# Two attentions on one core: context loads and key stores move ahead of other stores on SyncE's queue

## The chip, the cores and the metric

The kernel runs on one core of a Trainium2 chip, as one launch. The metric is the device time of that launch in microseconds. The kernel before takes 874.25 us, the median of three runs (872.12 to 876.36).

Engine names are those of the profile: PE multiplies matrices (PEld is its weight load), DVE is VectorE, ACT is ScalarE, POOL is GpSimd, SP is SyncE. SP issues most DMAs here. It works through one list of instructions in order: where it meets a semaphore wait, everything behind the wait stands.

## What is computed

Two layers work on `x` [16, 100, 256], with a context `ctx_1024` [16, 361, 256]:

```python
x = x + tanh(g_xattn[0]) * L0_xattn(layernorm(x), ctx, mask)   # 16 heads of 16, bias on q, k, v, o
x = x + tanh(g_ffn[0])   * L0_ffn(layernorm(x))                # 8 experts, top 2, and a shared one
x = x + tanh(g_xattn[1]) * L1_xattn(layernorm(x), ctx)         # no mask, no bias but b_o
x = x + tanh(g_ffn[1])   * L1_ffn(layernorm(x))                # 8 LoRA experts, top 1

# both cross-attentions, for each batch b:
q = ln(x) @ Wq;  k = ctx @ Wk;  v = ctx @ Wv
out = softmax(q k^T / sqrt(16)) v @ Wo
```

Everything is float32 to the caller.

## The kernel before

The kernel is written by hand engine by engine: each engine has its own instruction stream and all order between engines is by semaphores. The two attentions share their code; `l` is 0 or 1. Batches are numbered 0 to 15, and buffers that hold one batch's data exist twice (`cT[n % 2]`, `KS[n % 2]`, `QS[n % 2]`, `V1[n % 2]`).

**What a batch needs.** `ctx_load(l, n, p)` (L384) brings the transposed context of batch n, 361 KB, into `cT[p]`. PE projects it to keys (`project_k`, L2067, two halves m) and to values (`project_v`, L2085, three tiles of rows). Keys are kept as three bfloat16 parts for accuracy: ACT writes the first (`k_first`, L973), DVE the remainder `kr` (`k_rest`, L1555), ACT the second (`k_second`), POOL the third (`k3`, L724). They lie in one buffer `kp`, so ACT's `k_first` of batch n waits until the store of the keys of n-1 has landed. `k_store(l, n)` (L400) stores `kp` to the scratch tensor `scr_k` in three DMAs of 180.5 KB, each behind the wait for its part. `k_load` (L415) brings them back in the layout that the scores want, as two halves of three DMAs each into `KS`, behind a wait for the store (half 0). Queries go the same way: `q_store(l, g)` (L472) stores one group in six DMAs, `q_load` (L463) brings the queries of one batch into `QS` behind a wait for that store. A group is four batches in the first attention and two in the second. `max_load` (L519) brings the negated row maxima into `QS`, behind ACT's copy `mp`.

`ctx_load` waits for `v_ready` >= START + 2(n-1): the values of batch n-2, which used the same buffer, are projected.

**The steady state.** Step b (PE: L2166) holds the transposed scores and the weighted sum of batch b, the scores and maxima of batch b+1, the values of batch b+2 (tiles 0 and 1 at the end of step b, tile 2 near the start of step b+1) and the keys of batch b+3 (in the second half). Steps have u = b % 2: "odd steps" are those with u = 1. SP's step (L544) is: context b+3; in even steps 2 to 12 of the second attention the store of query group b/2 + 1; k_load and q_load of b+2, half 0; max_load of b+1 and a wait for its landing; k_load and q_load of b+2, half 1; the masks (first attention); the key store of b+3.

**The prologues.** SP's `attn` (L577) writes out the order of the first batches. First attention: ... context 2, Wo, q_store(0), q_store(1), k_store(1), loads of keys and queries 1, small vectors, max_load(0), k_store(2), masks 2, q_store(2), step 0. Second: ... context 2, k_store(1), q_store(0), loads of keys and queries 1, max_load(0), k_store(2), q_store(1), step 0. In both, DVE computes `kr` of keys 2 and then `cTl`, the low part of context 1 (`ctx_low`, L1548), which PE's values 1 wait for; DVE then takes the last maxima of batch 0 and splits them, and PE transposes them (`turn_max`, L2109) between tiles 1 and 2 of values 1.

The profile gives matrix multiplications issued through `split_mm` the line L1962.

Of the kernel before, what the change touches and what calls it, by code (L numbers as in the profile page):

```python
# [15 lines left out]
B, S, S2, D, H = 16, 100, 361, 256, 16  # L16
# [54 lines left out]
def build(nc, io, out):  # L71
    ctx = ExitStack()
    with ctx:
# [309 lines left out]
        def _(sp):  # L383
# [135 lines left out]
            def max_load(l, n, p):  # L519

                sp.wait_ge(sa[l]["mp"], START + n + 1)
                sp.sem_inc(s_held, 1)
                sp.dma_start(QS[p][SROWS:KSROWS, :, :], mp[:, :]).then_inc(sd["mload"][p], 16)
# [18 lines left out]
                sp.dma_start(woT[:, t:t + 2, :], io["woT"].rearrange("(t p) n -> p t n", p=P)[:, t:t + 2, :]).then_inc(s_wf[1], 16)  # L542

            def step(l, b, u, i, has_ctx, has_k, weights=None):  # L544
                if has_ctx:
                    ctx_load(l, b + 3, 1 - u, False)
                if l == 1 and u == 0 and 2 <= b <= 12:
                    q_store(l, b // 2 + 1)
                if has_k:
                    k_load(l, b + 2, 0)  # L550
                    q_load(l, b + 2, 0)
                    if l == 0 and b == 0:
                        q_store(l, 3)
                    if l == 0 and weights is not None:
                        expert_up(weights, u)
                        expert_down(weights, u)
                    if l == 1 and 8 <= b < 12:
                        inner_weights(b - 8)
                    if l == 1 and b == 12:
                        outer_weights(0)  # L560
                        outer_weights(1)
                    max_load(l, b + 1, 1 - u)
                    sp.wait_ge(sd["mload"][1 - u], 16 * (i + u + 1))
                    sp.sem_inc(s_held, 1)
                    k_load(l, b + 2, 1)
                    q_load(l, b + 2, 1)
                    if l == 1 and b == 13:
                        outer_weights(2)
                        outer_weights(3)
                        for r in range(LPROD):  # L570
                            sp.dma_start(BT[r * LR:(r + 1) * LR, :], io["loraBT"]).then_inc(s_wf[1], 16)
                if l == 0 and has_ctx:
                    mask_load(b + 3, 1 - u, False)
                if has_ctx:
                    k_store(l, b + 3)

            def attn(l):  # L577
# [14 lines left out]
                if l == 0:  # L592
                    for part in range(NPIECE):
                        first_keys(part, (0, 1))
                    first_queries(l, 0)
                    first_queries(l, 1)
                    ctx_load(l, 2, 0, False)
                    sp.dma_start(w_attn[0]["o"][:, :, :], io["L0_xattn_Wo"].rearrange("(k p) n -> p k n", p=P)).then_inc(s_wa[0]["o"], 16)
                    restore_rows(l)
                    q_store(l, 0)  # L600
                    q_store(l, 1)
                    k_store(l, 1)
                else:
                    k_store(l, 0)
                    for half in range(2):
                        k_load(l, 0, half)
                    first_queries(l, 0)
                    ctx_load(l, 2, 0, False)
                    first_queries(l, 1, (1, 2))
                    k_store(l, 1)  # L610
                    q_store(l, 0)
# [3 lines left out]
                if l == 0:  # L615
                    small_vectors()
                max_load(l, 0, 0)
                k_store(l, 2)
                if l == 0:
                    mask_load(2, 0, False)  # L620
# [1973 lines left out]
```

## Time and profile before

| | |
|---|---|
| median of three runs | 874.25 us (872.12 to 876.36) |
| the profiled execution | 885.38 us, its span 883.2 us |
| mean granted TensorE clock in it | 0.953 |
| PE busy | 790.0 us, 89% of the span |
| DVE, ACT, POOL busy | 577.6, 472.0, 213.8 us |
| DMA | 117.85 MB, mean 133 GB/s |
| idle PE before `project_k`, released by a context's landing | 9.9 us, 10 times |
| idle ACT before `kp`, released by the landing of `scr_k` | 5.7 us, once |

The first attention runs from the start to about 320 us, its feed-forward layer to 466, the second attention to about 765, the last feed-forward layer to the end. Stretches of time in the rows are in us from the start of the span. "Released by" is what ended an idle time. In a row in order of time the figures are start, duration, engine, line, operation, output and input; a bracket at the end is the idle time before it. Rows of matrix multiplications that overlap are merged, and ends are modelled.

### The profile page before, as it was taken

To read this page: it belongs to the slowest core of one execution; us is meant where nothing else is said; L and a number is where in the kernel's file an instruction comes from. 1 tells how busy PE (TensorE), PEld (TensorE's weight loads), DVE (VectorE), ACT (ScalarE), POOL (GpSimd) and SP (SyncE) were. 2 spreads that over 40 slices of the span, in tenths; PEclk is the share of its full clock that TensorE was granted. 3 is DMA by queue.
4 is the path that set the end of the run, shared out by engine and by line. 5 is a ranking of instruction groups with operands and counts; after the bars stand their busy time and mean duration, and the time that the engine had idled before them with its cause. 6 is when DMAs were issued, how large, how long until landed. Compare 5 with 4: busy or idle time off the path is not lost.

```text
span 883.2 us, 22331 instructions
## 1 busy us (share of the span) xinstructions
PE 790.0 (89%) x7992; PEld 608.7 (69%) x7992; DVE 577.6 (65%) x1773; ACT 472.0 (53%) x1012; POOL 213.8 (24%) x212
## 2 busy tenths in 40 slices
PE   5869999999999887799997788999999889898996
PEld 2546777777767664489974566776776667576996
DVE  3757777777777766465546767778788657564332
ACT  2436566556556566246652455666566555654553
POOL 2535132133223306400026522332221111000000
PEclk9889999999999999799997889999999999799998
DMA  7698878878886906523326958699789877000001
GB/s 195 159 192 189 171 150 169 160 152 179 160 175 131 221 2 174 147 75 120 121 75 161 175 126 171 139 184 176 149 176 187 159 172 165 2 1 1 19 19 37
DMA packets 153754, 117.85 MB, mean 133 GB/s; under 512 B 81564, under 2 KB 145160, under 8 KB 153640
## 3 DMA queue, kind: packets, MB, share of 16 engines
q1 hardware_dynamic: 146400, 107.93, 57.1%
q0 software_dynamic: 4096, 6.57, 3.0%
q10 hardware_dynamic: 3152, 1.96, 0.9%
q8 instruction: 64, 1.05, 0.6%
q14 instruction: 42, 0.34, 0.2%
HBM read 76.17 MB, written 38.30 MB: 130 GB/s over the span
## 4 chain that ended last, share of the span: by engine, by line
PE 57%; DMA 15%; SPq 9%; DVE 7%; issue 4%; ACT 4%; ACTq 1%; another core or an unknown queue 1%; POOL 0%; DVEq 0%
PE ps L1962 18%; PE ps L2080 7%; DMA cT<-in_ctxT 7%; PE ps L2106 5%; PE ps L2139 4%; PE ps L2129 4%; DMA scr_q<-qp 3%; SPq L477 3%; DMA QS<-mp 3%; PE ps L2400 3%; PE ps L2125 3%; SPq L426 2%; PE ps L2163 2%; SPq L413 2%; PE ps L2033 2%
## 5 line engine op out<-in xcount | busy, mean ns | idle before, releaser
L1017 ACT ACTIVATE prob<-ps 128x400 f32<-128x400 f32 (+1 forms) x384 | 182.5, 500 | 96.3 <-PE ps L2129 83.0
L2106 PE MATMUL ps<-KS,QS 96*100 96x361 bf16 x512 | 166.3, 341 | 17.0 <-DMA QS<-scr_q 5.8
L1575 DVE CUSTOM_DVE_ANT_0 ps<-ps,biasq 100x361 f32<-100x361 f32 x256 | 135.4, 543 | 52.1 <-PE ps L2106 48.4
L1579 DVE TENSOR_REDUCE mx<-ps 100x1 f32<-100x361 f32 x256 | 127.4, 528 | 59.4 <-PE ps L2106 56.6
L2129 PEld LDWEIGHTS ps<-QS,KS 98*128 98x128 bf16 x1536 | 109.3, 100 | 50.1 <-issue 10.8
L2129 PE MATMUL ps<-QS,KS 98*128 98x100 bf16 x1536 | 134.0, 211 | 6.0 <-ACT prob L1017 3.8
L2080 PE MATMUL ps<-cT,wk 128*128 128x361 f32 x256 | 102.5, 512 | 17.6 <-DMA cT<-in_ctxT 9.9
L2106 PEld LDWEIGHTS ps<-KS,QS 96*100 96x100 bf16 x512 | 64.1, 127 | 54.7 <-DVE mx L1579 13.4
L727 POOL TENSOR_TENSOR kp<-kr,kp 128x722 bf16<-128x722 f32 x32 | 48.7, 1523 | 195.9 <-ACT kp L988 195.6
L2139 PE MATMUL ps<-prob,V 128*17 128x100 f32 (+1 forms) x3072 | 80.4, 253 | 1.4 <-ACT xT L908 1.4
L2139 PEld LDWEIGHTS ps<-prob,V 128*17 128x17 f32 (+1 forms) x3072 | 65.1, 98 | 12.9 <-issue 8.0
L2080 PEld LDWEIGHTS ps<-cT,wk 128*128 128x128 f32 x256 | 48.8, 207 | 36.4 <-issue 14.9
L1962 PE MATMUL ps<-wvh,cTh 128*128 128x256 f32 x192 | 61.5, 320 | 5.9 <-DVE cTl L1552 5.4
L2125 PE MATMUL ps<-biasT,ident_bf 128*128 128x400 bf16 (+1 forms) x192 | 64.2, 334 | 2.0 <-ACT prob L1017 1.8
L983 ACT ACTIVATE kp<-ps,bk 128x361 bf16<-128x361 f32 x64 | 35.3, 554 | 55.3 <-PE ps L2080 46.9
L848 POOL DMA_INDIRECT scr_x<-xn,posi x32 | 33.3, 1041 | 93.8 <-PE ps L2139 87.0
L1962 PE MATMUL ps<-wvl,cTh 128*128 128x256 f32 x192 | 55.1, 287 | 0.0
L1962 PE MATMUL ps<-wvh,cTl 128*128 128x256 f32 x192 | 55.0, 287 | 0.0
L1560 DVE SCALAR_TENSOR_TENSOR kr<-ps,bk,kp 128x361 f32<-128x361 f32 x64 | 37.7, 592 | 22.6 <-ACT kp L983 21.9
L1824 DVE TENSOR_TENSOR hlo<-hh,hhi 128x400 fp32r<-128x400 f32 x32 | 18.4, 575 | 49.2 <-ACT hhi L1262 49.1
L1962 PEld LDWEIGHTS ps<-wvh,cTh 128*128 128x128 f32 x192 | 37.6, 196 | 12.1 <-DVE kr L1560 6.1
L1834 DVE TENSOR_TENSOR hx<-ps,sg 128x192 f32<-128x192 f32 (+1 forms) x48 | 17.1, 357 | 42.9 <-ACT sg L1183 36.3
(225 smaller groups left out, 1612.9 us busy)
## 6 DMA issues: line engine op xcount, KB each, us to landing
scr_k<-kp SPq DMA_DIRECT2D x93, 180.5 KB
KS<-scr_k SPq DMA_DIRECT2D x62, 270.8 KB
cT<-in_ctxT SPq DMA_DIRECT2D x32, 361.0 KB
KS<-scr_k SPq DMA_DIRECT2D x62, 180.5 KB
QS<-scr_q SPq DMA_DIRECT2D x60, 150.0 KB
KS<-scr_k SPq DMA_DIRECT2D x62, 90.2 KB
scr_q<-qp SPq DMA_DIRECT2D x42, 100.0 KB, 6.6
xg<-scr_x SPq DMA_DIRECT2D x32, 128.0 KB
```

What stands on the lines that cost most here:

```text
L727: nc.gpsimd.tensor_tensor(kp[:, 2, :, :], kr[:, :, :], kp[:, 1, :, :], ALU.subtract).then_inc(a["k3"], 1)
L983: nc.scalar.activation(kp[:, 0, m, :], ps[:, key_bank(l, n, m), 0:S2], ACT.Identity, bias=bk[l][:, m:m + 1]).then_inc(a["k1"], 1)
L1017: nc.scalar.activation(prob[0:KROWS[t], t, hg, :], ps[0:KROWS[t], c % 2, 0:HQ * S], ACT.Exp).then_inc(a["exp"], 1)
L1560: nc.vector.scalar_tensor_tensor(kr[:, m, :], ps[:, key_bank(l, n, m), 0:S2], bk[l][:, m:m + 1], kp[:, 0, m, :], ALU.add, ALU.subtract).th ...
L1575: nc.vector.tensor_tensor_reduce(ps[0:S, banks[h % len(banks)], 0:S2], ps[0:S, banks[h % len(banks)], 0:S2], biasq[p][:, :], 1.0, -3.0e38, ...
L1579: nc.vector.reduce_max(mx[:, h:h + 1], ps[0:S, banks[h % len(banks)], 0:S2], axis=AX.X).then_inc(a["max"], 1)
L1962: x = mm(dst, w_parts[wp], x_parts[xp], start=first and j == 0, stop=last and j == 2)
L2080: x = mm(ps[:, key_bank(l, n, m), 0:S2], w_attn[l]["k"][:, k, m * P:(m + 1) * P], cT[p][:, k, 0:S2], start=k == 0, stop=k == KT - 1)
L2106: mm(ps[0:S, banks[h % len(banks)], 0:S2], QS[p][0:SROWS, h, :], KS[p][0:SROWS, h * S2:(h + 1) * S2], start=True, stop=True).then_inc(a["s ...
L2125: mm(dst, ident_bf[0:rows, :], bc(biasT[p][0:rows, t, :].unsqueeze(1), [rows, HQ, S]), start=True, stop=False)
L2129: x = mm(ps[:, c % 2, j * S:(j + 1) * S], KS[p][:, h * S2 + t * P:h * S2 + (t + 1) * P], QS[p][:, h, :], start=l == 1, stop=l == 1 or j == ...
L2139: x = mm(ps[32 * j:32 * j + HD + 1, 6, hg * S:(hg + 1) * S], V1[p][0:KROWS[t], t, HQ * hg + j, :], prob[0:KROWS[t], t, hg, j * S:(j + 1) * ...
```

## The change

Three things change on SP's list, and nothing on any other engine. The same DMAs are issued, with the same waits and sizes.

In the prologue of the first attention k_store(1) stands ahead of q_store(1). In both prologues context 3 is loaded behind max_load(0), ahead of k_store(2), and no longer at the start of step 0. In the second attention an odd-numbered context b+4 is loaded at the end of the odd step b, ahead of its key store, and no longer at the start of the even step b+1. Even-numbered contexts there, and all contexts after number 3 in the first attention, stay where they were.

```diff
             def step(l, b, u, i, has_ctx, has_k, weights=None):
-                if has_ctx:
+                if has_ctx and b > 0 and (l == 0 or u == 1):
                     ctx_load(l, b + 3, 1 - u, False)
...
                 if l == 0 and has_ctx:
                     mask_load(b + 3, 1 - u, False)
+                if l == 1 and u == 1 and b + 4 < B:
+                    ctx_load(l, b + 4, u, False)
                 if has_ctx:
                     k_store(l, b + 3)
...
                     q_store(l, 0)
+                    k_store(l, 1)
                     q_store(l, 1)
-                    k_store(l, 1)
                 else:
...
                 max_load(l, 0, 0)
+                ctx_load(l, 3, 1, False)
                 k_store(l, 2)
```

## Rows read from the trace of the kernel before

**Rows 1.** The chain of waits, 30 to 62 us: start, duration, what.
```profile
43.94 4.68 DMA scr_k<-kp
...
51.42 2.90 PE ps L1962 x12
...
54.49 1.33 PE ps L1962 x6
```

**Rows 2.** SP's instructions in order of time, 39.5 to 44.6 us.
```profile
39.03 3.70 SPq L477 DMA_DIRECT2D scr_q<-qp  x7
42.84 1.55 SPq L413 DMA_DIRECT2D scr_k<-kp  x3
```

**Rows 3.** POOL, ACT, DVE and PE in order of time, 38 to 54 us.
```profile
38.56 1.46 POOL L727 TENSOR_TENSOR kp<-kr,kp 128x722 bf16<-128x722 f32 x1 [1.88 <-ACT kp L988]
...
42.11 0.84 ACT L891 ACTIVATE xT<-ps 128x800 f32<-128x800 f32 x1 [1.97 <-PE ps L1974]
...
45.91 0.14 DVE L1575 DVE_READ_ACCUMULATOR2_ANT mx<- 100x1 f32 x1
49.32 1.09 DVE L1560 SCALAR_TENSOR_TENSOR kr<-ps,bk,kp 128x361 f32<-128x361 f32 x2 [3.27 <-ACT kp L983]
...
53.59 0.17 DVE L1589 SCALAR_TENSOR_TENSOR mxs<-mx,mxb 100x16 f32<-100x16 f32 x1
...
51.42 0.55 PE L1962 MATMUL ps<-wvh,cTh 128*128 128x256 f32 x1 [4.53 <-DVE cTl L1552]
```

**Rows 4.** Busy time by stretch; after the engines: granted clock, DMA share, GB/s.
```profile
38.00:40.00 2.00, 2.00 (x9) 1.18 (x8) 2.00 (x9) 2.00 (x4) 1.44 (x2) 1.00 0.37 99
44.00:46.00 2.00, 2.00 (x8) 1.10 (x7) 1.64 (x8) 0.00 (x0) 0.00 (x0) 1.00 1.08 307
52.00:54.00 2.00, 2.00 (x11) 2.00 (x11) 1.93 (x10) 0.31 (x2) 0.80 (x1) 0.50 1.21 178
```

**Rows 5.** PE's first key projection of steps 0, 2, 6 and 12, second attention.
```profile
510.50 1.57 PE L2080 MATMUL ps<-cT,wk 128*128 128x361 f32 x2 [1.85 <-DMA cT<-in_ctxT]
...
547.47 0.88 PE L2080 MATMUL ps<-cT,wk 128*128 128x361 f32 x2 [2.60 <-DMA cT<-in_ctxT]
...
616.12 0.87 PE L2080 MATMUL ps<-cT,wk 128*128 128x361 f32 x2 [0.45 <-DMA cT<-in_ctxT]
...
719.22 1.57 PE L2080 MATMUL ps<-cT,wk 128*128 128x361 f32 x2 [1.45 <-DMA cT<-in_ctxT]
```

**Rows 6.** SP in order of time around context 3 and in step 2; PE's values 3.
```profile
501.78 0.61 SPq L390 DMA_DIRECT2D cT<-in_ctxT  x1
...
537.17 1.58 SPq L413 DMA_DIRECT2D scr_k<-kp  x3
539.04 0.58 SPq L390 DMA_DIRECT2D cT<-in_ctxT  x1
539.67 3.59 SPq L477 DMA_DIRECT2D scr_q<-qp  x6
...
550.09 0.57 SPq L469 DMA_DIRECT2D QS<-scr_q  x1
...
538.67 0.28 PE L1962 MATMUL ps<-wvh,cTl 128*128 128x256 f32 x1
```

**Rows 7.** The chain of waits, 514 to 522 us: values at the full clock.
```profile
517.82 1.62 PE ps L1962 x12
```

**Rows 8.** Busy time by stretch, 608 to 620 us; columns as in rows 4.
```profile
608.00:620.00 12.00, 11.29 (x115) 7.84 (x119) 9.96 (x25) 7.07 (x17) 3.15 (x5) 1.00 1.13 220
```

**Rows 9.** The chain of waits in step 6 of the second attention.
```profile
613.52 6.75 DMA scr_q<-qp
...
620.36 3.10 DMA QS<-scr_q
```

**Rows 10.** SP and ACT in order of time in step 6, 612 to 624 us.
```profile
615.58 1.25 SPq L426 DMA_DIRECT2D KS<-scr_k  x3
...
617.86 0.57 ACT L983 ACTIVATE kp<-ps,bk 128x361 bf16<-128x361 f32 x1 [1.87 <-PE ps L2080]
```

## The prediction

> **What bounds the kernel now.** I read the page first: PE is busy for 89% of the span, so only a stretch in which PE stands still or runs at the lower clock can give time back. The list of busy times does not say where those are. The chain of work that ended last does. In the first 60 us it does not stay on PE: it goes from SP's query stores to the store of the second batch's keys, the landing of that store, one ScalarE copy, two VectorE steps, and only then to PE's value projection [rows 1]. Then I read the lists in order of time around the three places that the diff touches: the prologue of the first attention, that of the second, and the steps of the second.
>
> The prologue of the first attention. The store of keys 1 begins at 42.84, behind seven query stores that hold SP from 39.03 to 42.73, the last of q_store(0) and all six of q_store(1) [rows 2]. Its last part, issued at 43.94, lands 4.68 us later [rows 1]. ScalarE has been free since 42.95; VectorE stands 3.27 us for ScalarE's copy, and PE 4.53 us for VectorE [rows 3]. PE then works at half of the full clock (0.50 granted, the 1.2 GHz level) [rows 4].
>
> The second attention. PE waits for a context at 510.50 (1.85 us, step 0), 547.47 (2.60, step 2), 616.12 (0.45, step 6) and 719.22 (1.45, step 12) [rows 5]. All four are odd-numbered contexts, those that even steps load. Their issue lies right behind a key store: in step 2 keys from 537.17, the context at 539.04, six query stores from 539.67 [rows 6].
>
> **The change part by part. (a) Keys 1 ahead of queries 1, first attention.** Nothing is added; three DMA issues move ahead of six. The six take 42.73 less 39.03, times six sevenths, 3.2 us, so k_store(1) begins at about 39.6. Its third part needs POOL's subtraction, done at 38.56+1.46 = 40.02 [rows 3], and its issue would come at 40.7, so SP does not stand. When does it land? The DMA engines were at share 0.37 in 38 to 40 and at 1.08 and 307 GB/s in 44 to 46 [rows 4]: at 39.6 the queue is nearly empty. 541 KB at 307 GB/s are 1.8 us, and the last part is issued at 40.7, so its bytes are through at about 41.6. Before, bytes still ran at full rate up to 46, and the landing was at 48.62, at most 2.6 us later. So the landing comes at 44.2 or sooner. ScalarE is free at 42.95 and copies at about 44. Now VectorE is late instead: its maxima run until 45.91+0.14 = 46.05, and its kr step started at 49.32. **It starts 3.27 us earlier, bound by VectorE and no longer by the store**; the landing has 1.3 us of room before it would matter again. PE's wait of 4.53 becomes 1.26.
>
> The clock is the second term. With a stand of 1.26 instead of 4.53 I expect the full clock. 12 value matmuls take 2.90 us here [rows 1] and 1.62 at the full clock [rows 7]. The transposition of the maxima then has to wait for VectorE, 53.59+0.17-3.27 = 50.49 [rows 3], and PE goes on at 50.6 with the last 6 matmuls (1.33 here, 0.8 at the full clock), ending at 51.4 where they ended at 55.82 [rows 1]. **Sum of (a): 4.4 us**, or 3.3 if the clock falls anyway. What the query matmuls behind them save is some tenths and left out.
>
> On this the Trainium skill ("TensorE: Matmul & The Clock Gate", What's actually happening) says that the array is throttled by default and released by activity, and that the point of a change of level varies from run to run. By its rule PE keeps 2.4 GHz here or pays a low stretch elsewhere; the second gives 3.3. The row agrees with the first half: 0.50 after the long stand.
>
> What is queued behind: q_store(1) now ends at about 44.4, where k_store(1) ended. Its landing is wanted by q_first(3), after 55 in this trace; no cost. k_load(1), which waited for the landing, goes out at 44.5 instead of 48.7, and the small vectors, max_load(0) and keys 2 come four us earlier with it. That is needed, since PE is there over four us earlier.
>
> **(b) First context 3 ahead of k_store(2).** In the first attention the list shows no idle stretch of PE before keys 3; k_store(2) leaves 0.6 us later (a context takes 0.58 to issue [rows 6]), hidden by the wait of the k_load behind it for PE. Zero. In the second, the load leaves before three key stores (1.58) and six query stores (3.59) [rows 6], so at about 496.5 instead of 501.78. Its own wait, for values 1, is met within 1 us of max_load(0) ahead of it, which needs a transposition that PE does in the middle of them. It lands well before 510.50-1.85 = 508.65, where PE wants it. **Gain 1.85 us** [rows 5].
>
> **(c) Odd contexts ahead of the odd steps' key stores, second attention.** Here a wait moves with the issue. The load waits for the end of a value projection, which PE reaches inside its next step: 538.67+0.28 = 538.95 for the load of 539.04 [rows 6]. It cannot go out earlier than now. The key store, ready at 537.17, is held back by that wait and one issue, 2.5 us, and the query stores behind it by its three issues, 1.6. What is won is the place in the DMA queue: 541 KB of keys no longer precede 361 KB of context. In 608 to 620 the engines are saturated, at share 1.13 [rows 8]. At 220 GB/s the context lands 541/220 = 2.5 us earlier and the keys 361/220 = 1.6 us later.
>
> Step 2: the wait of 2.60 goes. But then another chain is late next: query stores, their landing, q_load, its landing, the next step's scores. In step 6 that is 613.52 plus 6.75, 620.36 plus 3.10 [rows 9], and PE starts its next step at 616.12+7.4 = 623.5, just as it lands. In step 2 q_load goes at 550.09 [rows 6], landing at 553.2; PE, coming 7.4 us and 1.3 of low clock after 547.47, was at 556.2. Now PE could be there at 552.3 and the load at 553.2 to 553.8. **Gain 2.5 us.** In step 12, by the same chain, I take **0.5** of 1.45. Steps 4, 6, 8, 10: waits of 0 to 0.45 go, but they are at the chain already, and each loses 0.5 us net: the query stores leave 1.6 later into a full queue, which absorbs most of it, and ScalarE's copy of the next keys, which waits for the key store's landing, wants it at 617.86 and would have it at 615.58+1.6 = 617.2 or later [rows 10]. **Loss 2.0**; the bounds of one such step are 0 (all absorbed) and 1.6 (none).
>
> **Sum**: 4.4 + 1.85 + 2.5 + 0.5 - 2.0 = 7.3 us. The profiled execution took 885.38 us (span 883.2, 2.2 around it), so it would take 878.1. It lies 11 us over the median 874.25, but the terms that are plain waits (3.27, 1.85, 2.60) do not hang on that. Against the median: 874.25 - 7.3 = **866.9**.
>
> **The rivals.** *Give-back*: (a) and (b) hold, but steps 2 to 12 lose the whole 1.6 us of the query stores' delay: 6 x 1.6 = 9.6 against 4.4 + 1.85 + 2.5. Time about 875, no change. For it: the chain of step 6 has no slack. Against: the engines there are saturated, so bytes and not issues set the landing. *Slower*: the held key store stalls ScalarE, and the exponentials queued behind its copy stop, and PE with them. In step 6 keys 8 had landed by 615.58, 2.3 us before the copy [rows 10]. If the delays add up (2.5 of issue and 1.6 of bytes) instead of overlapping, each of six steps stalls about 2 us, and such stands cost some 1.3 us of clock each, as 12 matmuls lose 2.90-1.62: 20 us, less 3.3 and 1.85: 889. It decides once the keys land over 2.3 us later than now. *The order of issue does not set the landing*: contexts land when they did, and (c) is only the loss of 2.0. 4.4 + 1.85 - 2.0 = 4.2, time 870. The Trainium skill ("DMA: Bandwidth & Descriptors", Queues, rings and completion order) says that descriptors of a ring are consumed in order while completion is not first in, first out. The landings of step 6 speak against the rival: keys by 615.58, context 616.12, queries 620.27, in the order of issue [rows 5, 9, 10]. *More*: nothing is given back and the clock holds too, with 1.3 us in each of steps 0 and 2: 4.4 + 3.15 + 3.9 + 1.45 = 12.9, time 861.4.
>
> **How the numbers follow.** Forecast 0.57, give-back 0.17, order without effect 0.07, more 0.13, slower 0.06. Range: 859 (more, with the 2 us by which the runs of before spread) to 874 (forecast and the lower half of give-back). A measurement of this kernel tells about 0.5%, 4.4 us, from no change: the line is at 869.9. Faster: the forecast, more and a little of the order case, 0.73. Within: 0.20. Slower: 0.07.
>
> **What would show it.** (a) VectorE's wait for ScalarE's copy gone, kr at about 46, PE's wait about 1.3, granted clock 1 behind it, values 1 done near 51.4. (b) No wait for a context at keys 3 of the second attention. (c) Waits for odd contexts under 0.3 us, the key store right behind the load, its landing some 2 us later, perhaps short ScalarE waits for it, more waits for queries at the start of odd steps. The prediction is wrong if step 0 of the first attention then waits for max_load or keys 1 as long as PE did before, or if the even steps of the second lose over 1.5 us each.

## The result, and the profile after

| | before | after |
|---|---|---|
| median, 20 runs each | 877.68 us (872.12 to 883.82) | 882.89 us (875.98 to 893.67) |
| ratio, 95% interval | | 1.0049 [1.0028, 1.0071] |
| profiled execution, its span | 885.38, 883.2 us | 893.67, 891.5 us |
| mean granted clock in it | 0.953 | 0.951 |

The change makes the kernel half a per cent slower, 4 to 5 us. The prediction said 7 us faster, and its range (859 to 874) does not hold the time. Of the 16.0 us between its 866.9 and 882.89, 3.4 are its starting point: the median of before was 874.25 over three runs and is 877.68 over twenty. The two profiled executions lie 7.7 and 10.8 us above the medians of their kernels, so they are read here for what happens in a step, and the sizes come from the ratios.

The table of idle times before PE's work moved from one line to the other. Before, PE lost 9.9 us in 10 waits for contexts. After, 2.0 us in 2 waits are left, both in the first attention, and these have grown:

```profile
PE ps L2109 <- DMA QS<-scr_q: 15.7, 10, 2.4
...
PE ps L1989 <- DVE xn L1334: 6.2, 8, 2.7
```

(Waits of PE after: line, what was waited for, us in total, times, longest. L2109 is the score, which was L2106 and had 5.8 us in 10 waits.) In the second attention PE no longer waits for contexts, it waits for queries. On SP the wait for the projected values, L389, grew to four times its length. First before, then after:

```profile
SPq L389 <- PE ps L1962: 5.0, 8, 1.5
```
```profile
SPq L389 <- PE ps L1965: 21.3, 13, 2.5
```

**The first prologue after.** ACT, DVE and PE in order of time, in answer to [rows 3], and SP to [rows 2]:

```profile
38.96 1.51 SPq L413 DMA_DIRECT2D scr_k<-kp  x3
40.52 3.20 SPq L477 DMA_DIRECT2D scr_q<-qp  x6
...
44.82 1.02 ACT L986 ACTIVATE kp<-ps,bk 128x361 bf16<-128x361 f32 x2 [2.20 <-DMA scr_k<-kp]
...
45.58 1.09 DVE L1563 SCALAR_TENSOR_TENSOR kr<-ps,bk,kp 128x361 f32<-128x361 f32 x2
...
47.68 0.36 PE L1965 MATMUL ps<-wvh,cTh 128*128 128x256 f32 x1 [1.11 <-DVE cTl L1555]
...
55.57 1.08 PE L2334 MATMUL ps<-wo,onT 128*100 128x256 f32 x4 [1.40 <-issue]
```

The keys go out first, ACT copies at 44.82, VectorE's `kr` follows its maxima with no wait, and PE stands 1.11 us instead of 4.53. The product with Wo starts at 55.57; before it was at 60.52, in the row of the same form

```profile
60.52 1.08 PE L2331 MATMUL ps<-wo,onT 128*100 128x256 f32 x4 [1.40 <-issue]
```

so 4.95 us are won up to there. Of that 4.0 us are still there at keys 3, 1.3 at keys 5 and 1.2 at keys 15 of the first attention. The clock did hold in 48 to 50 (1.00), but fell behind, as the second and third line of the busy times by stretch show (after the engines: granted clock, DMA share, GB/s):

```profile
48.00:50.00 2.00, 1.35 (x12) 1.15 (x10) 1.93 (x11) 0.57 (x2) 1.05 (x1) 1.00 0.98 182
...
60.00:62.00 2.00, 2.00 (x15) 1.30 (x14) 1.44 (x7) 1.61 (x4) 2.00 (x2) 0.61 1.13 260
62.00:64.00 2.00, 2.00 (x13) 1.14 (x11) 1.26 (x5) 1.13 (x4) 2.00 (x2) 0.53 1.12 320
```

**Step 6 of the second attention after.** SP in order of time, in answer to [rows 9, 10], from the second half of the loads of queries 7 to the load of queries 8:

```profile
609.80 0.57 SPq L469 DMA_DIRECT2D QS<-scr_q  x1
612.17 0.57 SPq L390 DMA_DIRECT2D cT<-in_ctxT  x1
612.94 1.55 SPq L413 DMA_DIRECT2D scr_k<-kp  x3
614.54 3.96 SPq L477 DMA_DIRECT2D scr_q<-qp  x6
620.13 2.21 SPq L426 DMA_DIRECT2D KS<-scr_k  x3
624.06 0.58 SPq L469 DMA_DIRECT2D QS<-scr_q  x1
```

The same piece of SP's list before:

```profile
607.39 0.58 SPq L469 DMA_DIRECT2D QS<-scr_q  x1
608.16 1.56 SPq L413 DMA_DIRECT2D scr_k<-kp  x3
609.84 0.58 SPq L390 DMA_DIRECT2D cT<-in_ctxT  x1
610.47 3.61 SPq L477 DMA_DIRECT2D scr_q<-qp  x6
615.58 1.25 SPq L426 DMA_DIRECT2D KS<-scr_k  x3
620.36 0.57 SPq L469 DMA_DIRECT2D QS<-scr_q  x1
```

From the first line to the last are 12.97 us before and 14.26 after. After, SP stands with nothing issued from 610.4 to 612.17, since the context's wait is now ahead of everything else. PE pays for it at the start of the next step, and its clock falls (PE in order of time, and busy time by stretch):

```profile
627.05 0.84 PE L2109 MATMUL ps<-KS,QS 96*100 96x361 bf16 x2 [2.21 <-DMA QS<-scr_q]
```
```profile
624.00:626.00 2.00, 0.84 (x8) 0.63 (x6) 1.10 (x3) 1.30 (x3) 1.60 (x1) 1.00 0.28 56
626.00:628.00 2.00, 0.95 (x4) 0.76 (x5) 0.37 (x1) 0.00 (x0) 1.51 (x3) 0.77 0.39 58
628.00:630.00 2.00, 2.00 (x9) 1.99 (x8) 0.60 (x2) 0.00 (x0) 1.82 (x2) 0.50 1.01 209
```

The odd steps 3 to 13 after begin with six such waits: 2.28, 2.37, 2.21, 2.20, 1.87 and 2.02 us. A seventh, of 0.95 us, lies within step 12.

### The profile page after: what moved, and what is told of

Same layout as the page of the kernel before. It is cut to its first block, busy times and chain, and to the rows that moved or that the text cites. A ratio compares the mean times of both kernels' runs of the same rounds, so it can differ in the third digit from the quotient of the medians.

```text
span 891.5 us, 22331 instructions
## 1 busy us (share of the span) xinstructions
PE 790.3 (89%) x7992; PEld 615.2 (69%) x7992; DVE 581.8 (65%) x1773; ACT 472.6 (53%) x1012; POOL 215.9 (24%) x212
## 3 DMA queue, kind: packets, MB, share of 16 engines
q8 instruction: 64, 1.05, 0.5%
## 4 chain that ended last, share of the span: by engine, by line
PE 56%; DMA 13%; DVE 10%; SPq 10%; issue 5%; ACT 4%; POOL 1%; DVEq 0%; ACTq 0%; POOLq 0%
PE ps L1965 18%; PE ps L2109 6%; PE ps L2083 6%; DMA scr_q<-qp 5%; PE ps L2132 5%; PE ps L2142 4%; SPq L477 3%; DMA QS<-scr_q 3%; PE ps L2166 2%; PE ps L2128 2%; DMA cT<-in_ctxT 2%; SPq L413 2%; PE ps L2024 2%; DMA QS<-mp 2%; DVE mx L1582 1%
## 5 line engine op out<-in xcount | busy, mean ns | idle before, releaser
L2109 PE MATMUL ps<-KS,QS 96*100 96x361 bf16 x512 | 169.1, 346 | 28.4 <-DMA QS<-scr_q 15.7
L2132 PEld LDWEIGHTS ps<-QS,KS 98*128 98x128 bf16 x1536 | 111.3, 102 | 54.0 <-issue 10.1
L2132 PE MATMUL ps<-QS,KS 98*128 98x100 bf16 x1536 | 136.4, 213 | 9.2 <-ACT prob L1020 4.9
L2109 PEld LDWEIGHTS ps<-KS,QS 96*100 96x100 bf16 x512 | 65.1, 129 | 65.0 <-DMA QS<-scr_q 17.2
L2083 PE MATMUL ps<-cT,wk 128*128 128x361 f32 x256 | 98.9, 497 | 9.5 <-PEq L2374 6.8
L851 POOL DMA_INDIRECT scr_x<-xn,posi x32 | 36.0, 1125 | 94.0 <-PE ps L2142 87.2
## 6 DMA issues: line engine op xcount, KB each, us to landing
scr_k<-kp SPq DMA_DIRECT2D x93, 180.5 KB, 5.2
KS<-scr_k SPq DMA_DIRECT2D x62, 180.5 KB, 4.2
```

The costliest lines, as they stand in the source:

```text
L851: nc.gpsimd.indirect_dma_start(scr_x, bass.IndirectOffsetOnAxis(posi[:, c, b:b + 1], 0), normalized(b), None).then_inc(s_scat, 16)
L2083: x = mm(ps[:, key_bank(l, n, m), 0:S2], w_attn[l]["k"][:, k, m * P:(m + 1) * P], cT[p][:, k, 0:S2], start=k == 0, stop=k == KT - 1)
L2109: mm(ps[0:S, banks[h % len(banks)], 0:S2], QS[p][0:SROWS, h, :], KS[p][0:SROWS, h * S2:(h + 1) * S2], start=True, stop=True).then_inc(a["s ...
L2132: x = mm(ps[:, c % 2, j * S:(j + 1) * S], KS[p][:, h * S2 + t * P:h * S2 + (t + 1) * P], QS[p][:, h, :], start=l == 1, stop=l == 1 or j == ...
```

## The experiments

**The parts one by one.** Four kernels each hold one part of the change, or two.

e1_a, part (a) alone:

```diff
                     q_store(l, 0)
+                    k_store(l, 1)
                     q_store(l, 1)
-                    k_store(l, 1)
```

> The kernel before with one edit: k_store(1) ahead of q_store(1) in the prologue of the first attention. Theory 'the prologue gain holds': PE reaches the Wo product of the prologue 4.9 us earlier, as in the trace of the changed kernel (55.57 against 60.52), and the whole kernel is 4 to 5 us faster, ratio 0.995. Theory 'eaten inside the first attention': the first scores are as early, but the keys of steps 1 to 3 give it back (in the changed kernel 4.0 us at keys 3, 3.2 at keys 4, 1.3 at keys 5, 0.7 to 1.2 at keys 14 and 15), and the kernel is 0.5 to 1.5 us faster, ratio 0.998 to 1.

Measured: 0.9988 [0.9950, 1.0027], medians 874.48 and 877.45. The mechanism is there as in the change, PE's wait is 2.20 us (46.11, for `cTl`) instead of 4.53, but the time is not to be told from no change.

e2_ab, parts (a) and (b), the steps of the second attention as before:

```diff
             def step(l, b, u, i, has_ctx, has_k, weights=None):
-                if has_ctx:
+                if has_ctx and b > 0:
                     ctx_load(l, b + 3, 1 - u, False)
...
                 max_load(l, 0, 0)
+                ctx_load(l, 3, 1, False)
                 k_store(l, 2)
```

> Keys 1 ahead of queries 1, and context 3 ahead of k_store(2) in both prologues; the odd contexts of the second attention stay at the start of even steps. Theory 'the queries' chain is the cost': without the held key stores the loss is gone, no wait for QS over 1 us at the start of an odd step, and the kernel is 1 to 4 us faster than before. Theory 'the early context is part of the cost' (it delays the landing of max_load(0), or a DVE step collides): slower than the kernel with keys 1 alone by 1 us or more, with PE waiting over 2 us between 495 and 510 again, as in the changed kernel (3.33 and 2.67).

Measured: 0.9981 [0.9939, 1.0022]. The point is a gain of 1.7 us; the 6.25 us that the prediction gave to both parts would be 0.9929, just outside.

e3_c, part (c) alone: the two lines of the diff for the odd contexts of the second attention, nothing in the prologues.

```diff
+                if l == 1 and u == 1 and b + 4 < B:
+                    ctx_load(l, b + 4, u, False)
                 if has_ctx:
                     k_store(l, b + 3)
```

> Only the odd contexts of the second attention move, ahead of the odd steps' key stores. Theory 'the queries' chain is the cost': PE gains 2.6 us at keys 5 and loses about 2.2 us at the start of each of the steps 3, 5, 7, 9, 11, with a low stretch of the clock behind each, 9 us from keys 5 to keys 15 as in the changed kernel; the kernel is 6 to 8 us slower than before, ratio 1.007 to 1.009. Rival 'the loss comes from the other edits or from the clock alone': within 2 us of before.

Measured: 1.0119 [1.0066, 1.0172]. This part alone loses 10 us, more than the whole change does, where the prediction had a gain of 1.0.

e4_b1, part (b) in the second attention alone.

```diff
                 max_load(l, 0, 0)
+                if l == 1:
+                    ctx_load(l, 3, 1, False)
                 k_store(l, 2)
```

> Only context 3 of the second attention moves ahead of k_store(2). Theory 'a wait saved': the 1.85 us wait at keys 3 goes and keys 3 start 1 to 2 us earlier against the start of the second attention, kernel 1 to 3 us faster. Rival 'another wait takes its place': as in the changed kernel PE waits over 2 us for xn or for the maxima's load and keys 3 start no earlier; kernel the same within 1 us.

Measured: 1.0006 [0.9963, 1.0049]: nothing, though the wait of 1.85 us is gone.

**What in part (c) costs: the held store or the order of the bytes?** e5_hold leaves the loads where they were and only makes SP wait, ahead of the odd steps' key store, for the event for which the moved context load waits. (The `sem_inc` is a free counter that nobody reads.)

```diff
+                if l == 1 and u == 1 and b + 4 < B:
+                    sp.wait_ge(sa[l]["v_ready"], START + 2 * (b + 3))
+                    sp.sem_inc(s_held, 1)
                 if has_ctx:
                     k_store(l, b + 3)
```

> The kernel before, all loads where they were; in the odd steps 1 to 11 of the second attention SP waits ahead of the key store for the value projection that the following context load waits for anyway. So the key store, and all behind it, leave as late as with the moved contexts, but nothing stands in front of the keys in the DMA queue. Theory 'the hold is the cost': the query stores leave 1.8 to 2.2 us later, the stands at the start of odd steps are as long as with the moved contexts or longer (2 us and more), the contexts land later as well, and the kernel is 8 to 14 us slower, ratio 1.01 or more. Rival 'the bytes of the context ahead of the keys are the cost': 0 to 3 us slower.

Measured: 1.0079 [1.0044, 1.0115]. The hold by itself, with the order of all transfers unchanged, costs time. But half of what was expected did not come: the stands of 2 us for queries at the start of odd steps are missing. PE's waits for queries are 1.11 us at most from step 2 on, and it stands for the odd contexts instead, which the hold delays here too, for 1.99, 1.73, 1.85, 0.69, 0.38 and 1.28 us:

```profile
PE ps L2083 <- DMA cT<-in_ctxT: 9.8, 11, 2.0
```

So this loss reaches PE another way than that of part (c), and the run does not say which share of part (c)'s loss is the hold.

Then the queries, whose lateness is what PE feels in the change, were moved forward. e6_c_q_before_k is part (c) with the order context, queries, keys:

```diff
-                if l == 1 and u == 0 and 2 <= b <= 12:
-                    q_store(l, b // 2 + 1)
...
+                if l == 1 and u == 1 and 1 <= b <= 11:
+                    q_store(l, (b + 1) // 2 + 1)
                 if has_ctx:
                     k_store(l, b + 3)
```

> Odd contexts moved as in the change, and the six query stores of an even step moved with them, to between the context load and the key store. The queries then leave as early after the context as before the change, the key store 3.6 us later still. Theory 'the queries' chain is the cost': the stands for QS at the start of odd steps fall under 1 us, unless the keys' store takes their place: ScalarE's copy of the next keys waits for its landing (here 3 to 4 us longer) and k_load too; I expect ratio 1.00 to 1.01. Theory 'the key store's landing is the cost': ScalarE waits 3 us and more per even step, PE stands behind it, ratio over 1.012.

Measured: 1.0190 [1.0138, 1.0241]. PE's waits for queries fall to 8.0 us in all, but now the keys are late and ScalarE stands, six times for 3.8 to 4.8 us in the second attention:

```profile
619.08 0.57 ACT L985 ACTIVATE kp<-ps,bk 128x361 bf16<-128x361 f32 x1 [4.81 <-DMA scr_k<-kp]
```

In the change itself the waits of this kind are 1.4 to 2.7 us in the second attention. Before, ScalarE stood for PE at the same places: 1.3 to 1.9 us in steps 4 to 10, over 4 us in steps 2 and 12.

e7_c_q_early has the order queries, context, keys, all in the odd step (the stores of the even step are taken out as in e6):

```diff
+                if l == 1 and u == 1 and 1 <= b <= 11:
+                    q_store(l, (b + 1) // 2 + 1)
                 if l == 1 and u == 1 and b + 4 < B:
                     ctx_load(l, b + 4, u, False)
```

> Odd contexts moved as in the change, and the query stores moved ahead of them, into the stretch in which SP would stand for the value projection (the queries' third part is ready 6 us before). Order in an odd step: query stores, context, key store. Theory 'the queries' chain is the cost': the stands for QS are gone, keys 5 start 2 us and more earlier, the contexts may wait for 600 KB of queries (up to 2.7 us); ratio 0.992 to 1.000. Rival 'the held key store is the cost': still slower than before by 5 us or more.

Measured: 1.0158 [1.0118, 1.0198]. The six query stores are in the queue during the hold, so a queue with work in it is not enough: contexts are as late as before (11.4 us of PE's waits) and ScalarE waits 23.8 us for keys.

e8_q_early is the kernel before with only the query stores moved to the odd step, ahead of the key store; nothing is held.

```diff
-                if l == 1 and u == 0 and 2 <= b <= 12:
-                    q_store(l, b // 2 + 1)
...
+                if l == 1 and u == 1 and 1 <= b <= 11:
+                    q_store(l, (b + 1) // 2 + 1)
                 if has_ctx:
                     k_store(l, b + 3)
```

> The kernel before, with the query stores of the even steps moved to the odd step before, ahead of its key store; contexts stay. Theory 'the queries' chain is what is late in the even steps': the small stands for QS of the kernel before (0.27, 0.34, 0.88 us) go, but key store and context leave 3.6 us later behind the query stores, and PE stands for the context in even steps by 1 to 3 us: ratio 0.998 to 1.006. If the chain had slack and only the hold made it late, this kernel shows no gain at all.

Measured: 1.0251 [1.0205, 1.0297], the slowest of all, and far outside what was expected. No wait for queries is left in the steps, and PE waits for contexts instead:

```profile
PE ps L2080 <- DMA cT<-in_ctxT: 21.7, 8, 3.9
```

In these three kernels each transfer that was put ahead took its time from another one that PE or ScalarE then stood for.

**Taking away the hole.** If SP's stand is what costs, keys that are issued ahead of it must save the loss. e10_two_parts_first is part (c), but two of the three parts of the keys go ahead of the context and the third behind it. PE gets its odd contexts early all the same. (The lines stand against e3_c, and `k_store` now takes the parts that it stores.)

```diff
                 if l == 1 and u == 1 and b + 4 < B:
+                    k_store(l, b + 3, range(2))
                     ctx_load(l, b + 4, u, False)
-                if has_ctx:
+                    k_store(l, b + 3, range(2, 3))
+                elif has_ctx:
                     k_store(l, b + 3)
```

> The moved contexts of the change (second attention only), but two of the three parts of the keys go ahead of the context; only the third part and what follows it are held. The prologues are as before. Theory 'the DMA engines run dry during the hold': with two parts of 181 KB in the queue they do not, so the bytes are through earlier; the stands for QS at the start of odd steps fall from 2.2 to about 1.2 us and the loss from 1.2% to about 0.5%. Rival 'the six query stores are issued later, and that is all': they leave only 1 us earlier than with the whole store held, loss 0.8 to 1.2%.

Measured: 0.9990 [0.9958, 1.0022]. The whole loss of part (c) is gone. What differs between the two kernels is when two DMAs of 180.5 KB are issued.

The rival of the expectation, the issue time on SP alone, is part of it: the two issues take 1.01 us in which SP would have stood, and the queries are stored 4.02 us after the last query load (mean of the even steps 2 to 12), against 4.99 in e3_c. It is not all of it: the next query load leaves 1.7 us earlier than in e3_c, and even 0.4 us earlier than in e1, e2 and e4, where these steps are untouched and the queries are stored at 3.55. A third thing goes as well: in e3_c ScalarE waits six times, 10.0 us in all, for the landing of keys in the steps of the second attention, and here never. The runs do not tell what each of the three is worth.

e15_one_part_first sends one part ahead (`range(1)` and `range(1, 3)` in the same diff):

> Part (c) alone, with one of the three parts of the keys issued ahead of the context and two behind it: a dose between the two kernels run so far (no part ahead: 1.0119; two parts ahead: 0.999). Theory of the hole: one part is 180 KB, at 220 to 300 GB/s 0.6 to 0.8 us of transfer, against a hole of some 2 us, so about a third to a half of the loss goes: 1.004 to 1.009, and the load of queries of the next step leaves at about 13.0 us behind the half-1 load in step 6 (no part ahead 13.59, two ahead 12.26). Rival (it is the late landing of the last part that counts, whatever the queue holds): as with two parts ahead, 0.996 to 1.002, or as with none, 1.010 to 1.014.

Measured: 1.0023 [0.9985, 1.0060], against 1.0119 and 0.9990. It lies between, nearer to two parts than I expected: by the middle values one part of keys saves 0.96 of 1.19%, not a third to a half, but the intervals are wide enough for a half. From the half-1 load to the next query load at step 6 are 13.23 us, where 13.0 was expected.

The DMA engines show what happens to the queue. Busy time by stretch (last two numbers: DMA share, GB/s) of the change, with the hold from 610.4 to 612.17:

```profile
609.00:611.00 2.00, 1.84 (x20) 1.47 (x19) 1.92 (x7) 1.30 (x4) 1.92 (x3) 1.00 0.96 214
611.00:613.00 2.00, 1.99 (x23) 1.67 (x21) 1.76 (x6) 1.70 (x5) 1.53 (x2) 1.00 0.99 144
613.00:615.00 2.00, 1.85 (x13) 1.32 (x14) 2.00 (x6) 1.50 (x4) 1.03 (x1) 1.00 0.63 128
615.00:617.00 2.00, 2.00 (x38) 1.27 (x36) 1.37 (x4) 1.01 (x3) 0.00 (x0) 1.00 1.07 340
```

The same place in the kernel before:

```profile
609.00:611.00 2.00, 1.90 (x20) 1.48 (x19) 1.77 (x5) 1.70 (x6) 1.48 (x3) 1.00 1.11 191
611.00:613.00 2.00, 1.94 (x14) 1.37 (x14) 1.81 (x5) 1.08 (x3) 0.76 (x1) 1.00 1.20 177
613.00:615.00 2.00, 1.90 (x37) 1.21 (x35) 1.64 (x4) 1.31 (x4) 0.00 (x0) 1.00 1.11 229
```

and in e10_two_parts_first, SP's list and the stretches:

```profile
599.13 0.58 SPq L469 DMA_DIRECT2D QS<-scr_q  x1
599.89 1.01 SPq L413 DMA_DIRECT2D scr_k<-kp  x2
601.70 0.84 SPq L390 DMA_DIRECT2D cT<-in_ctxT  x1
602.64 0.54 SPq L413 DMA_DIRECT2D scr_k<-kp  x1
```
```profile
601.00:603.00 2.00, 1.90 (x23) 1.49 (x21) 1.80 (x5) 1.70 (x5) 1.53 (x2) 1.00 1.09 197
603.00:605.00 2.00, 1.94 (x14) 1.21 (x11) 1.57 (x5) 1.26 (x4) 0.60 (x1) 1.00 1.06 230
```

About 3 us after SP stops issuing, the change's DMA share falls to 0.63, and in e3_c to 0.70 (612 to 614). Where two parts of keys are in the queue, and SP stands for 0.8 us instead of 1.8, it stays at 1.06 or more. That is the hole.

e14_change_two_parts_first is the whole change with this one difference:

> The whole change, but in the odd steps of the second attention two of the three parts of the keys are issued ahead of the odd context and only the third behind it. Theory (the loss is the hole in the DMA queue while SP stands for the end of the value projection with nothing issued): the loss of the change goes, as it went with part (c) alone, and what is left is the small gain of (a) and (b): ratio 0.995 to 1.000. From one half-1 load of queries to the next load of queries at step 6 about 12.3 us, where the change has 14.26. Rival (the changed order of bytes or the collisions in the second prologue make the loss, not the hold): 1.004 or more, as the change itself.

Measured: 0.9957 [0.9916, 0.9998], 869.0 against 872.89. The change as it stands is at 1.0049 [1.0028, 1.0071]; moving two DMA issues in front of a wait, in each of six odd steps, is worth 0.9%. This is also the fastest version tried. Its interval leaves 1 out by very little, so that it beats the kernel before is likely and not more; that it beats the change is clear.

**Are early contexts worth anything?** e11_c5_only moves the context of step 2 alone, the one where PE had waited longest:

```diff
+                if l == 1 and u == 1 and b == 1:
+                    ctx_load(l, b + 4, u, False)
                 if has_ctx:
                     k_store(l, b + 3)
```

> Only context 5 moves, the one for which PE waited longest (2.60 us in the trace of before; 1.7 to 2.2 in the traces of two other kernels with this stretch unchanged). Theory 'the query chain takes the wait over at once': keys 5 start 1.5 to 2.5 us earlier, step 3 begins no earlier or later by up to 2 us behind a stand of 2 us for QS; kernel 0 to 2 us slower. The prediction's theory: 2.5 us faster.

Measured: 1.0016 [0.9971, 1.0062]. The place where the prediction saw 2.5 us gives none that can be measured, though the interval just reaches that gain. In the trace PE does not wait for context 5, and step 3 begins with a stand of 1.66 us for queries. From keys 4 to keys 6 are 34.34 us, and 34.02 to 36.07 in e1, e2 and e4.

e12_odd_ctx_on_act and e13_a_all_ctx_on_act take the loads off SP, so that no wait for values holds anything on SP's list. ScalarE issues them behind its copy of the values: the odd contexts 5 to 15 in the first, contexts 4 to 15 and part (a) in the second.

```diff
-                if has_ctx:
+                if has_ctx and not (l == 1 and b > 0 and u == 0):
                     ctx_load(l, b + 3, 1 - u, False)
...
                 if has_b:
                     v_copy(l, b + 1, 1 - u, 1)
+                if (l == 1 and b > 0 and u == 0) and b + 3 < B:
+                    act.wait_ge(sa[l]["v_ready"], START + 2 * (b + 2))
+                    act.dma_start(cT[1 - u][:, :, 0:S2], io["ctxT"][b + 3]).then_inc(sd["ctx"][1 - u], 16)
```

> The kernel before, but the odd contexts 5 to 15 of the second attention are issued by ScalarE on its own DMA queue, right behind its copy of the last value tile, which waits for the same event as the load. SP is held by nothing and issues one DMA less. Theory 'holding SP was the cost of an early context, its place ahead of the keys was not': no wait of PE for an odd context, stands for QS as small as before, 3 to 7 us faster, ratio 0.992 to 0.997. Rival 'the engines have no bytes to spare: a context that comes earlier makes keys and queries land later by as much': waits for contexts go, stands for QS of 1 us and more appear, ratio 0.998 to 1.005. ScalarE gives up some 0.6 us per even step for the issue; if that shows, PE waits for prob.

Measured: 1.0028 [0.9994, 1.0063].

> Keys 1 ahead of queries 1 in the first prologue, and all contexts 4 to 15 of the second attention issued by ScalarE. Theory as in the run with the odd ones: the prologue's 1 to 3 us and 4 to 8 us in the second attention, since the even contexts (waits of 0.3 to 1 us per step) come earlier too: ratio 0.988 to 0.995. Rival: within 0.4% of before.

Measured: 0.9990 [0.9954, 1.0025]. In e12 PE's waits for contexts fell to 4.5 us in 5 places and those for queries to 3.9 us in 6, and the time did not. Part of the waits stayed: for context 5 alone PE waited 2.48 us in e12 and 3.21 us in e13. No kernel here shows that a wait for a context, once taken away, gives its length back.

**All of them by two numbers of the trace.** The first is the time from the last load of queries of one step to the first of the next, on SP, mean of the even steps 2 to 12. The second is PE's time from the start of keys 6 to that of keys 15, nine steps of the second attention.

| kernel | ratio | query load to query load | keys 6 to 15 |
|---|---|---|---|
| before | 1 | 12.77 | 153.5 |
| e1_a | 0.9988 | 12.54 | 150.9 |
| e2_ab | 0.9981 | 12.49 | 149.7 |
| e4_b1 | 1.0006 | 12.59 | 151.3 |
| e10, two parts ahead | 0.9990 | 12.15 | 147.5 |
| e14, change with two parts ahead | 0.9957 | 12.53 | 149.3 |
| e15, one part ahead | 1.0023 | 12.96 | 150.8 |
| e5_hold | 1.0079 | 13.25 | 155.1 |
| e3_c | 1.0119 | 13.86 | 157.3 |
| after | 1.0049 | 14.19 | 159.5 |
| e11_c5_only | 1.0016 | 12.46 | 148.6 |
| e12_odd_ctx_on_act | 1.0028 | 12.16 | 148.3 |
| e13_a_all_ctx_on_act | 0.9990 | 12.27 | 149.4 |
| e6, queries before keys | 1.0190 | 14.21 | 161.6 |
| e7, queries, context, keys | 1.0158 | 13.37 | 159.7 |
| e8_q_early | 1.0251 | 12.44 | 169.1 |

The last column for after is 725.77 less 566.25, in the rows of PE's first key projection

```profile
566.25 0.77 PE L2083 MATMUL ps<-cT,wk 128*128 128x361 f32 x2
...
725.77 0.77 PE L2083 MATMUL ps<-cT,wk 128*128 128x361 f32 x2
```

and for before 719.22 [rows 5] less the start of

```profile
565.74 0.88 PE L2080 MATMUL ps<-cT,wk 128*128 128x361 f32 x2
```

Each is one execution, and that of before took 7.7 us more than its median: e1, e2 and e4, which leave these steps alone, take 150.6 on average. Apart from the last three rows a later query load goes with longer steps, in rough order. The last three break it: there PE or ScalarE stands for contexts or keys. In e8 the query load is early and the steps are the longest of all.

## Why the prediction was wrong

**The bound.** That the first prologue hangs on the store of keys 1 was right: with the store early, PE's product comes 4.95 us sooner. That PE's waits for contexts in the second attention set its time was not. They were visible idle time, but the query chain stood right behind them, and the prediction charged it 0.5 us a step, in steps 4 to 10 alone. The trace also had four waits for even contexts, 0.42 to 0.95 us, which no part of the change touches.

**(a), 4.4 us: right in mechanism, too large as a term.** The store began at 38.96 (39.6 said), `kr` at 45.58 (46.05), PE's wait was 1.11 (1.26), the clock held behind it, and 4.95 us were won at the Wo product. Only the landing, at 44.8, came later than the 44.2 named as its latest: the last part was issued at 40.04, so it took 4.8 us, as long as before (4.68). The queue was not as empty as the prediction took it to be: the DMA share was 0.64 in 38 to 40 and 1.08 in 40 to 42. The run of this part alone measured 1.05 us of gain, [-2.4, 4.4]. Two things shrink the term. First, the trace of before was an uncommonly bad one at this place: from the second half of keys 2 to the Wo product it takes 21.6 us, the ten other kernels with the old order here take 19.2 to 21.0, the five with the new one 17.0 to 18.1, so the saving at that point is about 2.8 on average. Second, it shrinks on the way: over the same traces 2.4 are left at keys 3, 1.8 at keys 5 and 1.45 at keys 15. In the trace of after PE waits 1.53 us for context 4 at 84.38, and the granted clock is 0.61 and 0.53 in 60 to 64, where it was 1.00 before; its low stretch was in 50 to 58 then. The Trainium skill ("TensorE: Matmul & The Clock Gate", What's actually happening) says that the point of a change of level varies from run to run. The rows fit that in part: e1, e2 and e14, with the early store too, have their low stretch in 58 to 64 as well, and e13 has none there. With the fallen clock the prediction had 3.3, still above what was measured.

**(b), 1.85 us: the wait went, the time did not.** The context was issued at 496.09 (about 496.5 said) and PE no longer waits for it. But in the trace of after two other waits of PE in this prologue are longer (POOL, DVE and PE in order of time):

```profile
499.74 0.51 PE L2132 MATMUL ps<-QS,KS 98*128 98x100 bf16 x4 [3.33 <-DMA QS<-mp]
...
503.61 2.48 POOL L742 TENSOR_TENSOR x_sb<-x_sb,gbo 100x512 f32<-100x512 f32 x2
...
502.95 3.65 DVE L1334 TENSOR_SCALAR xn<-x_sb,mean_var,rstd 100x256 f32<-100x256 f32 x2
...
506.40 0.90 PE L1989 MATMUL ps<-ident,xn 100*128 100x100 f32 x4 [2.67 <-DVE xn L1334]
```

The first was 1.50 in the trace of before, but it is 2.0 to 3.3 in eleven of the fourteen other kernels, also in those with an untouched prologue (3.06 in e3_c); here the one trace of before was a good one. It averages 3.0 in the four kernels that hold part (b) and 2.2 in the twelve that do not, so the early context may be behind some of it; no run shows that by itself. The second is a collision of VectorE with GpSimd, told below. It turns up in eight of the other kernels, six of them without part (b), and is missing in e2_ab, which has it; so it does not hang on this part. Measured alone, (b) makes the kernel 0.5 us slower, between 3.2 us faster and 4.3 us slower.

**(c), a gain of 1.0 us: the step that failed.** It is the sentence "the query stores leave 1.6 later into a full queue, which absorbs most of it". Its support was the mean share of 1.13 over twelve us [rows 8]. But the same move that delays the query stores empties that queue: while SP waits for the values it issues nothing, and what stood behind the wait is the key store that had kept the engines busy in these very us. The share of the change falls to 0.63 there. So the delay goes through: queries are stored from 5.13 us after the last query load instead of 3.26, and the next query load leaves 1.42 later on average (14.19 against 12.77), or 1.65 later than in e1, e2 and e4. The prediction had bounded one such step by 0 and 1.6 and took 0.5; the delay is at the upper end, and the low clock behind the stand comes on top (0.77 and 0.50 in 626 to 630). From keys 6 to keys 15 after and e3 take 6.0 and 3.8 us more than before, and 8.9 and 6.7 more than the three untouched kernels. Five even steps lie in between, so each loses 1.8 us after, over the 1.5 that the prediction itself had named as the sign of being wrong.

**Step 2, a gain of 2.5 us, is the same error again.** The wait of 2.60 went, and keys 5 come 2.52 sooner (544.95 for 547.47). But from keys 4 to keys 6, so over step 2 and the step behind it, before takes 565.74 - 529.00 = 36.74 and after 566.25 - 529.25 = 37.00. PE arrived half a us later than foretold, at 552.8, and the queries landed at 555.09, where the prediction let them land at 553.2 to 553.8.

**The rivals.** "Give-back" was nearest: it said that steps 2 to 12 lose the whole 1.6 us. It is right that the delay goes through, and close in size (9.6 us, where part (c) alone lost 10), though it left the clock out. It came out too fast because it held (a) and (b) to be worth over 6 us and step 2 another 2.5; with the measured 1.7 of e2 and without step 2 it would have given 874.25 - 1.7 + 9.6 = 882. That this is so near 882.89 is partly luck: its start was 3.4 us low. It got 0.17 because "the engines there are saturated" counted against it. "Slower" named another mechanism, ScalarE's stands for the keys. They are there (11.0 us in six waits of the second attention). Before, ScalarE stood for PE at the same places about as long or longer, which speaks against them as the main cost, and in e5 there are none in the steps and time is lost all the same. But they vanish in e10 together with the loss, so their share is not shown. In e6, where they are 3.8 to 4.8 us long, more is lost than in e3_c. "The order of issue does not set the landing" is refuted, since contexts do land earlier: in the second attention no wait for one is left. "More" did not happen.

What is shown is that the position of the key stores against the wait makes the loss: they behind it, 1.2% are lost; two of three ahead of it, none. What is still open: how much of that loss is the hole in the queue, how much SP's issue time and how much ScalarE's waits, how much of it comes through the clock, and why one part of keys (e15) seems to save more than a third. The 4 us between the sum of the parts (e2 with e3 gives 1.010) and the change (1.0049) lie within the intervals of these runs.

## What to carry to other kernels

When a DMA is moved forward past other issues on the same queue, its wait moves with it: count how long the issuing engine stands, and compare that with how many bytes are already in the queue. In this kernel the queue did not absorb the delay, because the delayed transfers were the ones that had filled it. If a wait has to go early, issue ahead of it what is ready and what the chain behind wants next; two of the three parts of the keys in front of the wait turned part (c) from 1.2% slower into no measurable loss. What is issued ahead has to be chosen: queries in that place (e7) still lost 1.6%. And an idle time in one trace is worth at most its distance to the next late input, averaged over several traces: none of the waits for contexts taken away here measurably returned its length.

## What was not expected of the hardware

**VectorE beside GpSimd.** A VectorE step of 100x256 elements, one input in SBUF, takes 0.41 us as a median in both kernels, and 3.3 us where two GpSimd additions, 2.48 us together, run beside it (durations in ns, min/median/max, after and then before):

```profile
L1334 DVE TENSOR_SCALAR xn<-x_sb,mean_var,rstd x32: 395/409/3307, 115.7 to 685.6; 100x256 f32<-100x256 f32 x32
```
```profile
L1331 DVE TENSOR_SCALAR xn<-x_sb,mean_var,rstd x32: 401/408/641, 117.0 to 679.3; 100x256 f32<-100x256 f32 x32
```

Before, the two missed each other by 0.6 us: `xn` had ended at 503.46 when GpSimd began at 504.04. The Trainium skill ("SBUF — State Buffer", SBUF: two separate sides) says that GpSimd and some kinds of VectorE instruction share one pair of ports, which is taken for the whole of an instruction and not divided. The rows are in keeping with it, since VectorE's two steps end at 506.60, after both of GpSimd's additions have ended at 506.09. So are the other traces: this addition and `xn` overlap in nine of sixteen, and there one step of `xn` takes 2.6 to 3.4 us; in the seven others none does. The rows do not show who took the ports first: the step's recorded start, 502.95, lies 0.66 us ahead of GpSimd's, more than the 0.41 us that it takes alone. For a comparison of kernels this means that a shift of some tenths of a us can cost or save 2.5 us far from the change.

**The DMA engines run dry quickly.** With the loads of keys and queries just issued, a stand of 1.8 us on the issuing engine was followed within 3 us by a fall of the share from 0.99 to 0.63. With 361 KB of keys issued ahead of the wait, and a stand of 0.8 us, it stayed at 1.06 or more.
